# Row maxima's bf16 part by a second maximum over the slots, and maxima 7 units ahead of a pair instead of 8

## The reference

```python
q = (x @ Wq).reshape(B, S, 2 * H, d).transpose(0, 2, 1, 3) * scaling
k = (x @ Wk).reshape(B, S, 2 * H, d).transpose(0, 2, 1, 3)
scores = jnp.einsum('bhqd,bhkd->bhqk', q, k)
scores = jnp.where(causal_mask, -jnp.inf, scores)
probs = jax.nn.softmax(scores, axis=-1)
attn_weights = probs[:, :, 0] - lam * probs[:, :, 1]
attn = jnp.einsum('bhqk,bhkd->bhqd', attn_weights, v)
```

## Time and profile before

| what | value |
|---|---|
| median of 3 runs | 447.87 us (447.37 to 450.23) |
| profiled execution | 445.42 us, span 443.7 us |
| TensorE busy | 397.9 us (90%) |
| VectorE busy | 401.0 us (90%) |
| ScalarE busy | 350.0 us (79%) |
| GpSimd busy | 225.6 us (51%) |
| mean granted clock of TensorE | 0.96 of 2.4 GHz |

### The profile page before, as it was taken

One profiled execution on the slowest core, in us unless ns is written; L12 is line 12 of the kernel. 1 busy time (PEld: TensorE's weight loads), 2 busy tenths in 40 slices (PEclk: granted clock), 3 DMA queues, 4 the chain that ended last, 5 costly groups with the idle time before them and its releaser, 6 DMA issues.

```text
span 443.7 us, 16577 instructions
## 1 busy us (share of the span) xinstructions
PE 397.9 (90%) x5720; PEld 186.4 (42%) x5721; DVE 401.0 (90%) x565; ACT 350.0 (79%) x732; POOL 225.6 (51%) x514
## 2 busy tenths in 40 slices
PE   5745999999999999999999999999999999999882
PEld 3512344444444444444444444444444444535552
DVE  1889899999999999999999999999999999674754
ACT  3620788889998989898989898989898998887243
POOL 7200132565656565656565555555555555558522
PEclk9965599999999999999999999999999999999997
DMA  5564254311111111111111111111111110000011
GB/s 140 183 219 143 75 192 146 97 50 51 51 52 48 48 48 48 48 48 48 48 48 48 48 48 48 48 48 48 48 48 48 48 50 26 28 3 2 0 49 47
DMA packets 21390, 28.44 MB, mean 64 GB/s; under 512 B 4960, under 2 KB 9952, under 8 KB 21232
## 3 DMA queue, kind: packets, MB, share of 16 engines
q1 hardware_dynamic: 20768, 27.58, 20.6%
q10 hardware_dynamic: 592, 0.46, 0.3%
HBM read 20.39 MB, written 9.47 MB: 67 GB/s over the span
## 4 chain that ended last, share of the span: by engine, by line
PE 61%; DVE 12%; issue 10%; ACT 10%; DMA 2%; SPq 1%; POOL 1%; DVEq 1%; ACTq 1%; POOLq 0%
PE acc L677 26%; PE mx L595 14%; DVE part_max L1133 9%; PE ex L647 8%; ACT e_buf L1028 8%; PE ex L685 3%; PE mx L604 2%; PE ex L631 2%; DMA wk_sb<-in_L_attn_Wk 1%; SPq L316 1%; DVE turn_max L1146 1%; PE mx L814 1%; PE mx L769 1%; PE mx L677 1%; POOL rs L545 1%
## 5 line engine op out<-in xcount | busy, mean ns | idle before, releaser
L1133 DVE TENSOR_REDUCE part_max<-mx 128x2 f32<-128x1024 f32 (+2 forms) x288 | 339.3, 1212 | 7.1 <-PE mx L595 2.1
L1028 ACT ACTIVATE e_buf<-ex 128x512 f32<-128x512 f32 x576 | 304.8, 600 | 39.3 <-PE ex L647 34.6
L516 POOL TENSOR_SCALAR_AFFINE_SELECT e_buf<-e_buf 128x256 f32<-128x256 f32 x256 | 100.7, 411 | 173.5 <-ACT e_buf L1028 173.4
L677 PE MATMUL acc<-e_buf,v_grp 128*32 128x256 f32 x2756 | 181.9, 353 | 7.0 <-ACT o_rows L955 3.7
L647 PE MATMUL ex<-qe,ke 26*128 26x512 bf16 (+3 forms) x768 | 145.9, 334 | 0.5 <-ACT e_buf L1028 0.3
L595 PE MATMUL mx<-km,qm 29*128 29x128 bf16 (+3 forms) x1280 | 117.5, 271 | 13.4 <-DVE part_max L1133 11.4
L677 PEld LDWEIGHTS acc<-e_buf,v_grp 128*32 128x32 f32 x2756 | 64.8, 109 | 60.1 <-issue 31.8
L595 PEld LDWEIGHTS mx<-km,qm 26*128 26x128 bf16 (+1 forms) x1280 | 41.7, 94 | 114.1 <-DVE part_max L1133 66.4
L647 PEld LDWEIGHTS ex<-qe,ke 26*128 26x128 bf16 x768 | 45.4, 91 | 22.0 <-ACT e_buf L1028 7.4
L499 POOL TENSOR_TENSOR r_rms<-sq_eps,minus_half 128x16 f32<-128x16 f32 x15 | 43.7, 2911 | 0.1
L604 PE MATMUL mx<-mask,pick 32*128 32x128 bf16 x512 | 25.9, 220 | 0.0
(11 more groups left out here) (137 smaller groups left out, 249.0 us busy)
## 6 DMA issues: line engine op xcount, KB each, us to landing
qm<-q_rows SPq DMA_DIRECT2D x32, 128.0 KB, 2.6
km<-k_rows SPq DMA_DIRECT2D x32, 128.0 KB, 2.7
qe<-q_rows SPq DMA_DIRECT2D x32, 128.0 KB, 2.5
ke<-k_rows SPq DMA_DIRECT2D x32, 128.0 KB, 2.7
q_rows<-part_q SPq DMA_DIRECT2D x6, 256.0 KB, 3.0
k_rows<-part_k SPq DMA_DIRECT2D x6, 256.0 KB, 3.0
q_rows<-part_q SPq DMA_DIRECT2D x6, 192.0 KB
k_rows<-part_k SPq DMA_DIRECT2D x6, 192.0 KB
```

Source lines behind the costliest of these rows:

```text
L516: pool.affine_select(out=e, in_=e, compare_op=ALU.is_ge, fill=0.0, base=0, pattern=[[0, PAIR], [1, P]], channel_multiplier=-1)\
L677: last = pe.matmul(out, v, e, start=first, stop=over, skip_group_check=True)
L1028: nc.scalar.activation(e_buf[:, b, i, :], ex[:, ex_slot(b, i) % EX_BANKS, :], ACT.Exp).then_inc(s["exped"], 1)
L1133: nc.vector.tensor_reduce(target, mx_of(n, pr, m)[:].rearrange("p s (a b) -> p s a b", a=a), AX.X, ALU.max).then_inc(s["maxed"], 1)
```

## The change

EARLY goes from 8 to 7: 16 units are made ahead of the first burst, and burst b does unit b + 7. `combine` makes two maxima over the same slots, one behind the other: `row_max` in fp32, and the bf16 part straight into `turn_max`, in place of the cast. `split_low` moves from behind the third unit after the pair's last to behind the second; with the shift of the units that is burst 3 as before, while `combine` is in burst 2 and not in 1.

```diff
-EARLY = 8
+EARLY = 7
...
             def combine(n, par):
 
                 dve.wait_ge(s["maxed"], NU * (n + 1))
-                nc.vector.tensor_reduce(row_max[:], part_max[par][:].rearrange("p j (q i) -> p (j q) i", i=MSLOTS),
-                                        AX.X, ALU.max).then_inc(s["combined"], 1)
-
-            def split_high(n):
-
-                dve.wait_ge(s["combined"], 2 * n + 1)
+                blocks = part_max[par][:].rearrange("p j (q i) -> p (j q) i", i=MSLOTS)
+                nc.vector.tensor_reduce(row_max[:], blocks, AX.X, ALU.max).then_inc(s["combined"], 1)
                 wait(dve, s["max_turned"], n)
-                nc.vector.tensor_copy(turn_max[:, 0], row_max[:]).then_inc(s["combined"], 1)
+                nc.vector.tensor_reduce(turn_max[:, 0], blocks, AX.X, ALU.max).then_inc(s["combined"], 1)
...
             late = {0: [(low, 6)], 1: [(low, 7)],
-                    NU: [(combine, 0, 0)], NU + 1: [(split_high, 0)], NU + 2: [(split_low, 0)]}
+                    NU: [(combine, 0, 0)], NU + 1: [(split_low, 0)]}
...
                 if m == NU:
                     combine(n + 1, 1 - pr)
                 if m == NU + 1:
-                    split_high(n + 1)
-                if m == NU + 2:
                     split_low(n + 1)
...
-            for b in range(NU - EARLY + 3):
+            for b in range(NU - EARLY + 2):
                 burst(NG - 1, 1, 0, b)
```

## The result

| | before | after |
|---|---|---|
| median | 447.87 us (447.37 to 450.23) | 441.38 us (441.16 to 442.23) |
| profiled execution (span) | 445.42 (443.7) | 441.16 (439.4) |

The ratio is 0.9861, 95% interval 0.9836 to 0.9887: faster by 1.4%, 6.2 us. The forecast was 443.4, its range 440.8 to 448.0. Between the two profiled executions the difference is 4.3 us, where the forecast's sum said 4.5; the medians differ by more, and experiment 12 shows what part of that is spread of the kernel before. Three runs of the kernel before (472 and 728 us) and one of experiment 6 (608 us) fell into a slower state and are in no ratio or range here.

A forecast was written before the change was run, and what follows sets the result against it. TensorE and ScalarE in a ring were taken to bound each pair, not VectorE's total. Terms -1.7 - 2.5 - 1.1 + 0.8 = -4.5 us took the profiled 445.42 to 440.9, on the median 443.4; range 440.8 to 448.0.

The forecast's parts named there:

- The ring of TensorE and ScalarE: In the loop, these two engines waiting on each other set a pair's length; VectorE adds 0.14 to 0.15 us with a reciprocal.
- The steady bursts: Masked units move one burst later, shortening burst 1 on TensorE: -0.085 us in each of some 29 pairs, -2.5 us.
- bound of -0.12 a pair: Largest steady saving allowed (-3.6 us), if burst 1 with 12 matmuls is as short as burst 0 less its wait.
- The second maximum: A bf16 maximum replaces VectorE's cast, ending TensorE's wait in pairs with a reciprocal: 12 pairs x 0.14, -1.7 us.
- the wait is gone: In pairs with a reciprocal, TensorE's unit in burst 5 no longer waits for VectorE (0.18 idle before), with little to spare.
- The rule of the Trainium skill: On VectorE a maximum costs more than a copy: 58 ns in each of 32 pairs, 1.9 us; held only where GpSimd is silent.
- The start: Ahead of the first score, one unit fewer saves 1.13 us and the extra maximum gives 0.05 back: -1.08 us.
- The end: In pair 30 the attention's turn (L761) must wait for the last maxima, as one unit comes back there: +0.8 us.
- B: Rival, chance 0.27: in the loop ScalarE takes up what burst 1 frees, or burst 3 loses as much; 445.9 us.
- C: Rival, chance 0.1: burst 3's scores queue behind all 16 matmuls of the masked unit, so the kernel is slower; 449.4 us.
- D: Rival, chance 0.08: VectorE's second maximum costs 0.29 or more beside GpSimd and unit 3 waits again; 445.1 us.
- E: Rival, chance 0.1: more gain, -0.12 a pair in burst 1 and an earlier clock rise of a burst or two; 441.5 us.

The follow-up runs named there:

- experiment 12: The kernel before run once more, unchanged, for a second profile: 447.92 us, ratio 0.9995.
- experiment 6: The kernel after with EARLY back at 8 and the low part behind the third unit, second maximum kept: 445.25 us, ratio 0.9959.
- experiment 4: The kernel after with two more maxima that nothing reads, 0.25 us of VectorE in each pair: 443.16 us, ratio 0.9912.
- experiment 3: The kernel after with its list of units rotated by one, masked units back in bursts 1 and 2: 445.92 us, ratio 0.9986.
- experiment 7: The kernel after with the reciprocal over 2 of 32 columns, most normalising factors left out: 440.66 us, ratio 0.9849.
- experiment 9: The kernel before, EARLY 8 and cast kept, with only its units reordered so masked ones lie in bursts 2 and 3: 440.75 us, ratio 0.9838.
- experiment 1: The kernel before with EARLY at 7 and the cast kept, cast and low part behind the second unit: 443.49 us, ratio 0.992.
- Experiment 5: The kernel after with the first turn and copy of the attention one burst later in pair 30: 439.83 us, ratio 0.9831.
- experiment 8: The kernel after with its units reordered so that the masked ones lie in bursts 3 and 4: 437.5 us, ratio 0.9777.

## Why the prediction was right, and where not

**The bound.** The ring of TensorE and ScalarE, with VectorE in the long pair only, held: experiment 4 gave 0.25 us of VectorE to every pair and only the long ones grew; experiment 3 took no work away from any engine and lost all but 0.35 of the 4.56 that the loop and its neighbours gained.

**The steady bursts (-2.5 forecast).** Right in its mechanism, the largest term of the sum, and too small. The pairs without a reciprocal and the written-out ones show it bare: 0.14 and 0.16 a pair, not 0.085. In the long ones bursts 0 to 3 are 0.14 shorter too (3.85 to 3.71). For 28 intervals that is 12 x 0.14, 5 of 0.14 on average written out, and 11 x 0.14 of the long ones: about -3.9. The size that was off is that of burst 1: it took 0.40, not 0.46. The forecast took it as equal to burst 0, whose second score waits for ScalarE, and kept a shorter one for its bound of -0.12 a pair. Burst 3 came as forecast (0.56 to 0.57). So a pair gets 0.17 from burst 1 and gives 0.03 back in burst 3, which is even beyond that bound.

**The second maximum (-1.7 forecast).** Its own cost was right: 0.13 us, beside selects too. Experiment 6 prices the step by itself at 0.85 over 28 intervals, and the loop after the change leaves -0.7 for it (4.56 less 3.9). So the term was twice too large, and this step of the forecast failed in two ways. First, "so VectorE costs the ring 0.14 to 0.15 us in a pair with a reciprocal" put the whole distance between the two kinds at unit 6 (3.93 against 3.78) down to VectorE; in experiment 7, where nothing waits for VectorE, 0.04 of it is still there, so VectorE's share was 0.10. Second, "the wait is gone" came true in every second such pair only. There unit 3 starts 1.21 after the copy and the pair takes 10.99, which is 0.10 less than with the masked units' 0.14 alone. In the others it starts 1.33 to 1.35 after it and the pair takes 11.04 to 11.05, so only 0.05 is saved; and in one pair (127.05) TensorE waits 0.36 for VectorE and 0.18 is lost. Over the 11 pairs: 6 x 0.10 + 4 x 0.05 - 0.18 = 0.6. VectorE itself stands idle for some 0.1 ahead of unit 0 in the pairs of the second sort; why is not shown. The longer low part (0.42 to 0.43) falls into the pairs of 10.99, so it is not what costs. In experiment 9 the cast is as good (0.16 in the long pair, where it took 0.38): the saving was one of place, not of kind. With the lead of 7 the place matters more (experiment 1: 0.56 for the cast), and there the second maximum is worth 2.2 us, 309.30 less 307.12.

**The rule of the Trainium skill.** The Trainium skill, "VectorE: DVE Perf Modes", section on the perf-mode tier table, by which a maximum is dearer than a copy (my estimate 58 ns), agrees with experiment 9 where no GpSimd instruction holds the cast: 0.07 to the next instruction against 0.13. Behind a select that has begun it is turned round (0.29 for the cast, 0.13 for the maximum), as forecast.

**The start (-1.08).** -1.09 from first unit to first exponential. TensorE's clock reached 2.4 GHz earlier, too: the window of 54 to 56 us shows 0.99 after (0.50 before, and 56 to 57 shows 0.85). The stretch from the first exponential to the first copy is 0.24 shorter. That is luck: in the second profile of the kernel before it is as short (16.47).

**The end (+0.8).** +0.98, with a wait of 0.88 at L761 where some 0.7 was forecast. Experiment 5 shows that it is this wait.

**The rivals.** B (the masked unit only moves) falls with experiments 1 and 3. C (scores behind all masks) falls: they start 0.01 after the first. D falls by the 0.21 of the second maximum; but over half of its price came in, by the wait of unit 3 that stays in every second long pair and by the 0.04 that was not VectorE's. E was nearest in the steady part, with its 0.12 a pair.

**The sum.** Between the profiled executions the forecast was 4.5 and the result 4.3. Part of that is luck: the term of the steady bursts was 1.4 too small and that of the second maximum some 1.0 too large, and they nearly cancel.

**The median.** The forecast took the 2.45 between the median and the profiled execution as carried over to the kernel after. It wasn't: all four runs after the change are at 441.2 to 442.2. Experiment 12 shows where such a 2.5 us lies in the kernel before; why the runs of after don't show it isn't known, and four runs are few.

What stays open: where the 0.04 between the two kinds of pair in bursts 4 to 7 arises (with the masked units in bursts 3 and 4, experiment 8, it is gone and the kinds differ by 0.08), why VectorE comes later in every second long pair, and what decides between the two kinds of end.

## What to carry to other kernels

When engines run in a ring, ask which stretch each engine sets alone, and put the heavy items of a free order elsewhere; here one line that reorders a list gave as much as the change, and with the heavy units one burst further on and the end mended it was 10 us. Price a small VectorE instruction by the instruction that GpSimd runs beside it, and when one moves, look up what it comes to stand beside, and whether anything waits behind it: the low part grew to 0.58 in experiment 7 and cost nothing. Measure by the distance of a mark that comes once a round, since busy shares and the chain's shares hardly moved here.

## What the runs showed of the hardware

- A copy with cast, SBUF to SBUF, of 16 elements per partition takes 0.16 us alone, 0.38 beside two selects of GpSimd and 0.56 beside its `o_scaled` (experiment 1); it ends within 0.05 us of GpSimd's instruction. The low part, a TENSOR_TENSOR with both inputs in SBUF, behaves likewise: 0.16 alone, 0.58 (experiment 7). But not every instruction of GpSimd holds it: beside the power in `r_rms` (L499, 2.91 us from 226.09) the low part at 226.71 takes 0.16. A TENSOR_REDUCE from the same memory takes 0.20 to 0.22 in all places.
- Two executions of one program differ by 1.7 us at the end, where TensorE's granted clock falls from 1.00 to 0.92 and 0.65 in two windows of 4 us in the one and stays at 1.00 in the other.
